# A graph pair kernel: similarities transposed by VectorE blocks and DMAs instead of TensorE, mask folded into the spread norms

## What is computed

```
h   = relu(layernorm(x))
z_l = h @ W_lang.T ; z_g = h @ W_grav.T ; v = h @ W_V.T
A_l = relu(cos_similarity(z_l)) * not_eye * adj
A_g = exp(-dist2(z_g) / (2 sigma^2)) * not_eye * adj
K   = w_l * A_l / rowsum(A_l) + (1 - w_l) * A_g / rowsum(A_g)
x   = x + (K @ v) @ W_O.T
h   = relu(layernorm(x))
x   = x + (adj*adj) applied over the nodes of h + bias
```

## Time and profile before

| | |
|---|---|
| time, median of 3 (lowest to highest) | 1269.06 us (1268.77 to 1270.68) |
| the profiled execution: time, span | 1269.61 us, 1267.7 us |
| mean granted TensorE clock | 0.996 |
| TensorE busy | 1241.2 us, 98% |
| VectorE busy | 1058.5 us, 83% |
| ScalarE busy | 694.5 us, 55% |
| GpSimd busy | 574.7 us, 45% |
| one group in the steady part | 37.73 us |

### The profile page before, as it was taken

One profiled execution on the slowest core, in us unless ns is written; L12 is line 12 of the kernel. 1 busy time (PEld: TensorE's weight loads), 2 busy tenths in 40 slices (PEclk: granted clock), 3 DMA queues, 4 the chain that ended last, 5 costly groups with the idle time before them and its releaser, 6 DMA issues.

```text
span 1267.7 us, 22572 instructions
## 1 busy us (share of the span) xinstructions
PE 1241.2 (98%) x6324; PEld 1039.6 (82%) x6324; DVE 1058.5 (83%) x1826; ACT 694.5 (55%) x1324; POOL 574.7 (45%) x964
## 2 busy tenths in 40 slices
PE   7999999999999999999999999999999999999996
PEld 6878888888888888888888888888888888888884
DVE  5678888988888988888898888898888898888777
ACT  5346555456645456655446655546655545654543
POOL 1115553434554434554434555444555443455433
PEclk9999999999999999999999999999999999999998
DMA  6232424342333343333343232344242444243201
GB/s 243 34 72 81 106 54 95 99 108 81 102 71 78 99 108 87 95 79 70 99 108 97 86 93 56 99 108 103 79 108 49 99 101 108 79 103 69 47 34 66
DMA packets 308894, 112.55 MB, mean 89 GB/s; under 512 B 269840, under 2 KB 269968, under 8 KB 308880
## 3 DMA queue, kind: packets, MB, share of 16 engines
q1 hardware_dynamic: 177360, 95.78, 27.2%
q10 hardware_dynamic: 131520, 16.60, 7.9%
HBM read 46.20 MB, written 33.62 MB: 63 GB/s over the span
## 4 chain that ended last, share of the span: by engine, by line
PE 93%; DVE 4%; ACT 1%; issue 1%; DMA 1%; POOL 0%; SPq 0%; DVEq 0%; ACTq 0%
PE ring L866 75%; PE p_ps L866 15%; PE p_ps L939 2%; PE kt_ps L879 1%; DMA h2f<-in_L_gnn_W_grav 1%; DVE x_out L688 0%; DVE bn L568 0%; DVE y_lo L557 0%; ACT h L379 0%; DVE bn L637 0%; DVE x_ring L631 0%; DVE y_lo L784 0%; DVE deg L602 0%; DVE v_lo L784 0%; DVE hT_lo L557 0%
## 5 line engine op out<-in xcount | busy, mean ns | idle before, releaser
L301 POOL TENSOR_TENSOR x_out<-x_ring,bias_sb 128x512 f32<-128x512 f32 x128 | 162.8, 1295 | 499.9 <-DVE bn L637 499.9
L866 PE MATMUL ring<-hT_hi,Lw_hi 128*128 128x512 f32 x640 | 256.9, 401 | 4.9 <-DVE hT_lo L576 2.1
L406 ACT ACTIVATE y_hi<-ring 128x512 fp32r<-128x512 f32 x256 | 148.3, 592 | 206.5 <-PE ring L866 203.7
L866 PE MATMUL ring<-hT_hi,Lw_lo 128*128 128x512 f32 x640 | 250.6, 392 | 0.0
L866 PE MATMUL ring<-hT_lo,Lw_hi 128*128 128x512 f32 x640 | 250.2, 391 | 0.0
L866 PE MATMUL ring<-MT_hi,hT_hi 128*128 128x512 f32 x512 | 203.0, 396 | 0.0
L557 DVE TENSOR_TENSOR v_lo<-ring,v_hi 128x512 fp32r<-128x512 f32 x128 | 88.5, 692 | 136.8 <-ACT v_hi L442 136.8
L866 PE MATMUL ring<-MT_hi,hT_lo 128*128 128x512 f32 x512 | 200.0, 391 | 0.0
L866 PE MATMUL ring<-MT_lo,hT_hi 128*128 128x512 f32 x512 | 199.9, 390 | 0.0
L308 POOL TENSOR_TENSOR h_lo<-h2f,h_hi 128x512 fp32r<-128x512 f32 x124 | 158.0, 1296 | 84.8 <-ACT h_hi L476 84.8
L557 DVE TENSOR_TENSOR y_lo<-ring,y_hi 128x512 fp32r<-128x512 f32 x256 | 169.2, 680 | 28.4 <-ACT y_hi L406 28.3
(11 more groups left out here) (160 smaller groups left out, 2537.0 us busy)
## 6 DMA issues: line engine op xcount, KB each, us to landing
x_ring<-in_x SPq DMA_DIRECT2D x32, 1024.0 KB, 5.5
out<-x_out SPq DMA_DIRECT2D x128, 256.0 KB, 2.2
h_turned<-h SPq DMA_DIRECT2D x248, 64.0 KB, 2.1
h_turned<-h ACTq DMA_DIRECT2D x248, 64.0 KB, 2.1
rn_cols<-rn_dram SPq DMA_DIRECT2D x31, 256.0 KB, 3.9
x_ring<-in_L_gnn_W_lang SPq DMA_DIRECT2D x4, 256.0 KB, 5.6
h2f<-in_L_gnn_W_grav SPq DMA_DIRECT2D x1, 1024.0 KB, 9.2
chain<-in_L_gnn_W_O SPq DMA_DIRECT2D x1, 1024.0 KB, 13.0
```

The source lines that it names most:

```text
L301: pool.tensor_tensor(x_out[:, b], x_rows(g, b), bias_sb[:, :], ALU.add).then_inc(x2b_ready, 1)
L406: act.activation(y[0][:, a, :, l], bank(n).rearrange("p (b m) -> p b m", b=GB), ACT.Copy)\
L866: mm = pe.matmul(out, lhsT, rhs, start=(k == 0), stop=(k == len(terms) - 1))
```

## The change

P is no longer transposed by TensorE, but in the last group. VectorE transposes its 32x32 blocks (`turn_p`, into `diag`, whose former content is used up by then), once for each of the two similarities (l = 0 and 1), SP stores each half to DRAM (`store_p`) and fetches it back with the blocks in place (`fetch_p`, four DMAs a half, into the first half of `h`), and VectorE adds (`sum_s(i, 1)`, `sum_s(i, 0)`), now after the outputs. GpSimd multiplies the spread norms by the mask (`mask_norms`), and VectorE's `mask_l` takes max(A, 0) times that in one pass, where `similarities` and `mask_l` were two. Orders move with it: on VectorE the block transposes of h go behind `combine` and by one y block; on ScalarE the exponential goes behind the second y_hi of the next group, and `shift` ahead of the h2 copies; on GpSimd `row_norms` goes ahead of the last two bias adds, and `mask_norms` between the second and third `h2_lo`.

```diff
             def spread_norms_turn_p(g):
+                store_p(g, 0)
                 sp.wait_ge(rn_step, RN_STEPS * g + 1)
                 sp.dma_start(rn_dram, rn[:, 0]).then_inc(rn_stored, 16)
                 sp.wait_ge(rn_stored, 16 * g + 16)
                 sp.dma_start(rn_cols[:, :, :], rn_dram.unsqueeze(0).to_broadcast([P, P, GB])).then_inc(rn_spread, 16)
+                store_p(g, 1)
+                fetch_p(g, 0)
+                fetch_p(g, 1)
...
+            def store_p(g, l):
+                sp.wait_ge(p_blocks, 2 * g + l + 1)
+                sp.dma_start(p_dram[l], P_blocks[:, l].rearrange("p j b q -> p j (b q)")).then_inc(p_stored[l], 16)
+            def fetch_p(g, l):
+                sp.wait_ge(p_stored[l], 16 * g + 16)
+                for j in range(NQ):
+                    sp.dma_start(P_turned[j * Q:(j + 1) * Q, l], p_dram[l][:, j].rearrange("(i r) e -> r i e", r=Q))\
+                      .then_inc(p_turned[l], 16)
...
+            def mask_norms(g):
+                pool.wait_ge(rn_spread, 16 * g + 16)
+                by_col = mask[:, :].unsqueeze(2).to_broadcast([P, P, GB])
+                pool.tensor_tensor(rn_cols[:, :, :], rn_cols[:, :, :], by_col, ALU.mult).then_inc(rn_masked, 1)
...
-                if not after:
-                    row_norms(i)
+                row_norms(i)
                 if before:
                     for b in range(GB // 2, GB):
                         add_bias(i - 1, b)
+                    for b in range(GB // 2):
+                        h2_lo(i - 1, b)
                 if after:
-                    row_norms(i)
+                    mask_norms(i)
                 if before:
-                    for b in range(GB):
+                    for b in range(GB // 2, GB):
                         h2_lo(i - 1, b)
...
                         act.wait_ge(turned, TURN * (g - 1))
+                        act.wait_ge(s_ready, 2 * g - 2)
...
+                        if before and n == 2:
+                            exponentials(i - 1)
...
+                    if b == 0 and after:
+                        shift(i)
                     if before and b == 0:
                         h2_copy(i - 1, 0)
                         h2_copy(i - 1, 1)
-                    if b == 0 and after:
-                        shift(i)
...
             def mask_l(g):
-                dve.wait_ge(a_ready, 3 * g + 1)
+                dve.wait_ge(rn_masked, g + 1)
+                dve.wait_ge(s_ready, S_STEPS * (g + 1))
+                dve.scalar_tensor_tensor(out=A[:, :, 0], in0=A[:, :, 0], scalar=0.0,
+                                         in1=rn_cols[:, :, :].rearrange("p m b -> p b m"),
+                                         op0=ALU.max, op1=ALU.mult).then_inc(a_ready, 1)
...
-                        if after and n == 4:
-                            turn_blocks(i + 1, 0)
-                            turn_blocks(i + 1, 1)
                         if before and n == 4:
                             combine(i - 1)
                         if after and n == 5:
+                            turn_blocks(i + 1, 0)
+                            turn_blocks(i + 1, 1)
+                        if after and n == 6:
                             turn_blocks(i + 1, 2)
                             turn_blocks(i + 1, 3)
...
                 squared_norms(i)
+                turn_p(i, 0)
                 for b in range(GB):
...
                     turned_lo(i + 1, b)
-                    if b == 2:
-                        sum_s(i)
+                    if b == 0:
+                        turn_p(i, 1)
                 if before:
                     for b in range(GB):
                         output(i - 1, b, n + b)
-                similarities(i)
+                sum_s(i, 1)
+                sum_s(i, 0)
                 mask_l(i)
...
+            def turn_p(g, l):
+                if l == 0:
+                    dve.wait_ge(sq_ready, 3 * g + 2)
+                    wait_for(dve, p_stored[1], 16 * g)
+                else:
+                    dve.wait_ge(p_shifted, g + 1)
+                dve.transpose(P_blocks[:, l].rearrange("p j b q -> p b j q"),
+                              P_sb[:, :, l].rearrange("p b (j q) -> p b j q", q=Q)).then_inc(p_blocks, 1)
+            def sum_s(g, l):
+                dve.wait_ge(p_turned[l], 16 * NQ * (g + 1))
+                turned_l = P_turned[:, l].rearrange("p i (b q) -> p b i q", b=GB)
+                dve.tensor_tensor(A[:, :, l].rearrange("p b (i q) -> p b i q", q=Q), turned_l,
+                                  P_sb[:, :, l].rearrange("p b (i q) -> p b i q", q=Q), ALU.add).then_inc(s_ready, 1)
...
-                    if b == (2 if after else 0):
+                    if b == 0 and not after:
                         pe.wait_ge(p_shifted, i + 1)
                         for k in range(2 * GB):
                             mm = pe.transpose(p_ps[:, k // 2, k % 2], P_sb[:, k // 2, k % 2], ident[:, :])
                         mm.then_inc(pt_done, 1)
-                        if not after:
-                            transposes_rn(i)
+                        transposes_rn(i)
```

More of the change, by code:

```diff
@@ L30, in gnn_pair @@
     RN_STEPS = 2
+    S_STEPS = 2
     blk = {ac: n for n, ac in enumerate(TRI)}
@@ L103, in gnn_pair @@
         h_turned = sb("h_turned", [P, GB, C, P])
+        P_blocks = diag.rearrange("p b l m -> p (b l m)").rearrange("p (l j b q) -> p l j b q", l=2, j=NQ, b=GB)
+        P_turned = h[:, 0:2].rearrange("p l (i e) -> p l i e", i=NQ)
         h_blocks = h[:, :, :].rearrange("p b (c j q) -> p j (b c) q", c=C, j=NQ)
@@ L115, in gnn_pair @@
         woT_parts = [w[:, :, :] for w in h2]
+        p_dram = [nc.dram_tensor(f"p_dram_{l}", [P, NQ, GB * Q], F32).ap() for l in range(2)]
         rn_dram = nc.dram_tensor("rn_dram", [P, GB], F32).ap()
@@ L165, in gnn_pair @@
         blocks_ready, turned = sem("blocks_ready"), sem("turned")
+        p_blocks = sem("p_blocks")
+        p_stored, p_turned = [[sem(f"p_{what}_{l}") for l in range(2)] for what in ("stored", "turned")]
         ht_hi, ht_lo = sem("ht_hi"), sem("ht_lo")
@@ L171, in gnn_pair @@
         diag_ready = sem("diag_ready")
-        rn_step = sem("rn_step")
+        rn_step, rn_masked, a_scaled = sem("rn_step"), sem("rn_masked"), sem("a_scaled")
         def passes(hi_lo_lhs, hi_lo_rhs):
@@ L209, in store_out, with spread_norms_turn_p @@
                                  x_out[:, b]).then_inc(out_stored, 16)
-            def spread_norms(g):
+            def store_p(g, l):
[6 more added lines that the diff above has]
+                      .then_inc(p_turned[l], 16)
+            def spread_norms_turn_p(g):
+                store_p(g, 0)
                 sp.wait_ge(rn_step, RN_STEPS * g + 1)
@@ L227, in iteration @@
                 if after:
-                    spread_norms(i)
+                    spread_norms_turn_p(i)
                 store_out(i - 1, first_use(i) + PER - GB)
@@ L246, in _ @@
             turn_h(1)
-            spread_norms(0)
+            spread_norms_turn_p(0)
             sp.wait_ge(w_split, 3 * C)
@@ L425, in iteration @@
                 if before:
-                    act.wait_ge(s_ready, i)
-                    act.wait_ge(diag_ready, 2 * i)
+                    act.wait_ge(s_ready, 2 * i)
                 for half in range(2):
@@ L439, in iteration @@
                     if not after and b == 1:
-                        exponentials(i)
+                        exponentials(i, 2)
                     act.wait_ge(v_done, GB * i + b + 1)
@@ L458, in iteration @@
                         h2_copy(i - 1, 3)
-                if after:
-                    exponentials(i)
             def h2_full(g, b, last=False):
@@ L482, in shift, with exponentials @@
                 e.then_inc(p_shifted, 1)
-            def exponentials(g):
-                act.wait_ge(s_ready, g + 1)
+            def exponentials(g, steps=1):
+                act.wait_ge(s_ready, 2 * g + steps)
                 act.activation(A[:, :, 1], A[:, :, 1], ACT.Exp, scale=inv_sig2).then_inc(exp_done, 1)
@@ L577, in turned_lo, with mask_l_last @@
                    .then_inc(ht_lo, 1)
[L579 to L586, removed]
             maskb = mask[:, :].unsqueeze(1).to_broadcast([P, GB, P])
             def mask_l(g):
-                dve.wait_ge(a_ready, 3 * g + 1)
+                dve.wait_ge(rn_masked, g + 1)
[3 more added lines that the diff above has]
+                                         op0=ALU.max, op1=ALU.mult).then_inc(a_ready, 1)
+            def mask_l_last(g):
+                dve.wait_ge(r_done, 1)
+                dve.wait_ge(s_ready, S_STEPS * (g + 1))
+                dve.tensor_tensor(A[:, :, 0], A[:, :, 0], r_ps[:, :, :], ALU.mult).then_inc(a_scaled, 1)
+                dve.wait_ge(a_scaled, 1)
                 dve.scalar_tensor_tensor(out=A[:, :, 0], in0=A[:, :, 0], scalar=0.0, in1=maskb,
@@ L600, in row_factors @@
             def row_factors(g):
-                dve.wait_ge(a_ready, 3 * g + 3)
```

(17 more changed lines are left out.)

## The result

The changed kernel takes 1292.0 us (1291.25 to 1292.75) against 1269.1 for the one before: ratio 1.018, interval 1.016 to 1.020. The profiled execution has a span of 1291.0 us at a granted TensorE clock of 0.994. The span grew by 23.3 us.

What follows compares the result with a forecast made beforehand. GpSimd's lengthened, colliding queue was expected to decide: 30 groups x 0.80 = +24.0 us, less 0.87 for the first group, gave about 1292 us from the median of 1269.06. The range was 1263 to 1308.

Steps and rivals of the forecast that it cites:

- GpSimd's start: GpSimd's power, after the squared norms' last instruction (0.17 with GpSimd idle), starts at 591.47, a gain of 1.62 us.
- Four collisions: All four hT_lo of VectorE meet working GpSimd, costing it 4 x 0.46 = 1.84 us; last h_lo ends at 603.35.
- 0.61 + 0.18: VectorE's chain a group: +0.61 us for half sums and masked pass behind the outputs, +0.18 for the combination awaiting ScalarE.
- DMAs: Spread norms land by 598.4 at worst, fetched half by 602 to 603.9 before its sum at 605; turned h covered.
- The 0.6 to spare: Margin between the spread norms landing (598.4 at worst) and GpSimd's mask multiplication starting no earlier than 599.0.
- The rival of VectorE alone: VectorE's chain decides, no collision costs GpSimd anything, h_lo 3 ends before 602.55: 1265.8 us; chance 0.2.
- The full 0.87: TensorE stays the bound and the 0.87 us a group of removed P transposes is kept: 1242 us; chance 0.03.
- The +0.80: Added us a group: the late last h_lo delays graph 3's first-layer product and the next group's first y block.
- this is what I expect to decide: GpSimd's queue, filled without a pause and delayed by collisions, was expected to set the time.
- an end of h_lo 3 within 11.3 us of sqc: Sign of a wrong prediction: GpSimd's last h_lo ending that soon after the squared norms' last instruction starts.
- the output behind the product and the hT_lo behind GpSimd reach the same figure: Graph 3's output held by its product, or hT_lo ending late behind GpSimd, also costs VectorE's chain 0.8 us a group.

Runs made afterwards that it cites:

- run 4: The changed kernel with every hT_lo computed from a PSUM tile in place of h_turned (low part of h meaningless): 1269.6 us.
- run 6: The changed kernel without GpSimd's mask multiplication and with only the last hT_lo (graph 3) computed from PSUM: 1267.3 us.
- run 7: The changed kernel without GpSimd's mask multiplication, all hT_lo from PSUM, and without the half sum of the l similarities: 1251.9 us.
- Run 1: The changed kernel without GpSimd's mask multiplication (l similarities left unmasked): 1293.4 us.
- runs 1, 2: Run 1, and the changed kernel with GpSimd's mask multiplication behind all four h_lo, nothing left out, at 1293.2 us.
- run 8: The kernel before with only GpSimd's mask multiplication behind its h_lo and VectorE's one masked pass; TensorE still transposes P: 1266.8 us.
- run 9: The kernel of run 8 with GpSimd's mask multiplication also waiting for the last hT_lo: 1280.7 us.
- run 10: The changed kernel with the mask multiplication behind the h_lo, and h_lo of graph 3 waiting for the last hT_lo: 1333.3 us.

## Why the prediction was right, point by point

The time (1292) and the group (38.5) came out as said, and so did most terms of the sum.

- **GpSimd's start.** sqc takes 0.17 with GpSimd idle and the power follows 0.25 after its start, as taken from the earlier trace rows.
- **Four collisions.** 0.46, 0.46, 0.37 (the multiplication, 1.47 against 1.10 alone; over all groups its median is 1.54) and 0.43: 1.72 in this group against 1.84 predicted. The multiplication itself is 1.10, not 1.25. The last h_lo ended at 603.15 on the clock of before, predicted 603.35; the next y block began at 604.07, predicted 604.19.
- **VectorE.** The masked pass is 1.09 (taken: 1.07), the half sums 1.28 for two. The combination starts where ScalarE's scaling ends, as said. The chain from the outputs to KT_lo grew by 0.82, against 0.61 + 0.18.
- **DMAs.** This was closer than said. The spread norms landed 4.4 us behind their issue, at 609.5 or 598.7, where I had taken 598.4 at worst; the multiplication could start at 598.75, where I had taken 599.0, since only two collisions lie ahead of it. The 0.6 to spare was nothing, and in 9 of 31 groups GpSimd waited for the norms: 6.05 in the first, 0.18 to 0.37 in the others. That it cost little is luck: in those eight others the multiplication then took only 1.14 to 1.33. The eight fetches took 5.51 us to issue, 0.69 each where I had taken 0.35; still the half sums waited for them only in the first group (0.95). The turned h had 5 us of cover in the kernel before, not some 10: its last DMAs are issued by 623.3 and land in 2.1, and hT_hi starts at 630.43. It was enough.
- **The rival of VectorE alone**, 1265.8 without collisions: run 4 gives 1269.6, run 6 1267.3. Nearly right; in run 4 GpSimd waits 1.07 for the spread, which I had not counted in that case.
- **The full 0.87** is not kept while VectorE carries both sums: runs 4 and 6 end near the time of before, and run 7, with one sum less, far below it.

The +0.80 itself was got along TensorE's way (h_lo 3, product of graph 3, first y block), while the length of the group is set along VectorE's: the fourth output held by that product, then a chain that is 0.82 longer. The prediction had noted that both give the same figure. That they agree so closely is luck: the first is the lateness of h_lo 3 against the product behind it, the second is the price of VectorE's passes on a start that the same h_lo holds where it was, and nothing in the change makes the two equal.

The part that was wrong is in the text on GpSimd and in the last part: "this is what I expect to decide", with an end of h_lo 3 within 11.3 us of sqc as the sign that the prediction fails. Run 1 has it at 10.84 and is no faster. The sentence a little further on, that the output behind the product and the hT_lo behind GpSimd reach the same figure, was the better one: there are two routes from the collisions to VectorE's chain, the fourth output held by h_lo 3, and the last hT_lo held by whatever GpSimd does at that moment. Closing one (runs 1, 2) leaves the other at the same price, which the arithmetic of that paragraph gave and its headline did not.

The Trainium skill, "SBUF — State Buffer", section "Who interferes with whom", says that a VectorE instruction with at most one SBUF input, outside the modes that use both of its ports, does not contend with GpSimd. Run 4 bears this out: the only thing changed in it is that hT_lo has one SBUF input in place of two. On VectorE's side the wait is full (hT_lo ends 0.54 to 0.56 behind GpSimd's end); on GpSimd's the cost was 0.37 to 0.46.

The same section of the Trainium skill calls the shared ports an exclusive lock. The prediction took that for the whole of both instructions and said that the trace agrees. For GpSimd's power it does not. In the kernel before, the power of 128x4 runs from 593.09 to 594.10, and an hT_lo that starts inside it takes no longer than alone:

```profile
593.42 0.68 DVE L576 TENSOR_TENSOR hT_lo<-h_turned,hT_hi 128x512 fp32r<-128x512 f32 x1
```

## What to carry to other kernels

Before filling an engine's hole, look at what the engine beside it does in that hole: here GpSimd's idle 2.65 us were part of what let VectorE's two-input instructions run at 0.68, and with the hole filled each collision put GpSimd back by 0.37 to 0.46. When an instruction is too long, ask whose end it follows before moving anything: the last hT_lo of run 8 followed h_lo 3 and not the multiplication beside it, and run 9 was built on the wrong one. Work taken off the busiest engine is a gain only by as much as the engine that receives it has slack on its own chain; find that by what gates the next product (KT_lo, 0.14 before it), not by busy shares. And where two routes lead from one delay to the path, an experiment that closes one of them shows nothing: close both, then each.

## What the runs showed of the hardware

- A small GpSimd instruction (0.20) took 1.14 beside VectorE's masked pass (1.09, two SBUF inputs), and ended 0.07 behind it (run 10): it pays 0.94 there, where a 128x512 GpSimd instruction pays 0.37 to 0.46 for an hT_lo of 0.68.
- GpSimd's power of 128x4 (1.01) does not hold an hT_lo that starts 0.33 or 0.34 behind its start: 0.68, as alone (kernel before; also for the hT_lo at 555.68 and at 631.17).
- GpSimd's multiplication of 128x512 by a broadcast mask in place took 1.10, less than the 1.29 of an add of the same size with two full operands.
- Issuing a fetch of 64 KB in 512-byte runs took SP 0.69 us (5.51 for eight), twice the 0.32 to 0.34 of the 256 KB store; the stores to DRAM landed in 3.2 us (median) where output stores of the same size land in 2.1, and behind the first of them the 2 KB of norms landed in 1.8, where it was 1.4.
